# Attention on one core: a third pair of score banks for the first 15 ticks, key remainders and early normalisation on GpSimd

## The reference

```python
H_l = H @ W_l
H_r = H @ W_r
S = H_l @ H_r.T
beta = jax.nn.softmax(S, axis=-1)
B = beta @ H
O = B @ W_h @ W_g
return adj @ H + gamma * O
...
x = _layernorm(x + _L3_gnn_ref(x, adj, ...), axis=-1)
```

## Time and profile before

| what | us |
|---|---|
| median of three runs | 1487.05 |
| the profiled execution: its own time | 1489.51 |
| its span, first to last instruction | 1487.7 |
| PE busy in the span | 1383.7 (93%) |
| DVE busy | 901.8 (61%) |
| ACT busy | 690.0 (46%) |
| GpSimd busy | 235.3 (16%) |

### The profile page before, as it was taken

One profiled execution on the slowest core, in us unless ns is written; L12 is line 12 of the kernel. 1 busy time (PEld: TensorE's weight loads), 2 busy tenths in 40 slices (PEclk: granted clock), 3 DMA queues, 4 the chain that ended last, 5 costly groups with the idle time before them and its releaser, 6 DMA issues.

```text
span 1487.7 us, 17011 instructions
## 1 busy us (share of the span) xinstructions
PE 1383.7 (93%) x5831; PEld 792.1 (53%) x5831; DVE 901.8 (61%) x1223; ACT 690.0 (46%) x871; POOL 235.3 (16%) x136
## 2 busy tenths in 40 slices
PE   5999999988899989989999999999799999999995
PEld 2444444422122223237777767777567676667753
DVE  2767666700000013358888887776888888888875
ACT  0100010111001102247777766665687887788776
POOL 0111111000000000001011000000233333333343
PEclk8999999999999999999999999999999999999998
DMA  9966655699999999998899988985000000000001
GB/s 347 356 242 253 236 226 226 209 373 408 407 403 409 408 404 406 408 373 296 309 325 315 315 294 299 318 301 196 0 1 1 1 1 1 1 1 1 1 1 57
DMA packets 101296, 339.40 MB, mean 228 GB/s; under 512 B 11371, under 2 KB 12907, under 8 KB 101099
## 3 DMA queue, kind: packets, MB, share of 16 engines
q1 hardware_dynamic: 101226, 338.50, 61.0%
HBM read 336.36 MB, written 2.10 MB: 228 GB/s over the span
## 4 chain that ended last, share of the span: by engine, by line
PE 58%; DVE 17%; DMA 14%; ACT 6%; issue 5%; SPq 1%; POOL 0%; DVEq 0%; ACTq 0%; POOLq 0%
DMA raw<-in_adj_s 13%; PE acc L1109 8%; PE acc L1170 6%; PE acc L1165 6%; PE acc L1166 6%; PE acc L1073 5%; PE acc L1193 4%; PE acc L1093 4%; DVE peak L858 4%; DVE rsum L686 4%; PE acc L1258 3%; DVE ring L882 3%; ACT ring L612 2%; ACT ring L600 2%; DVE t_lo L791 2%
## 5 line engine op out<-in xcount | busy, mean ns | idle before, releaser
L791 DVE TENSOR_TENSOR t_lo<-raw,t_hi 128x1024 fp32r<-128x1024 f32 x224 | 275.4, 1251 | 63.7 <-ACT t_hi L555 58.9
L555 ACT ACTIVATE t_hi<-raw 128x1024 fp32r<-128x1024 f32 x224 | 234.1, 1057 | 75.2 <-PE acc L1170 71.3
L1165 PE MATMUL acc<-t_hi,st_hi 128*128 128x512 f32 x448 | 201.7, 450 | 4.2 <-DVE st_lo L696 2.9
L476 POOL TENSOR_TENSOR ring_lo<-ring,p_hi 128x1024 fp32r<-128x1024 f32 x64 | 155.4, 2429 | 271.4 <-ACT p_hi L606 271.4
L1109 PE MATMUL acc<-raw,h_a 128*20 128x512 f32 x736 | 163.9, 607 | 20.5 <-DMA raw<-in_adj_s 20.3
L1073 PE MATMUL acc<-raw,x 128*128 128x512 f32 x384 | 177.1, 610 | 6.2 <-DMA raw<-in_adj_s 6.2
L500 ACT ACTIVATE at<-acc 128x512 f32<-128x512 f32 x48 | 28.7, 597 | 317.9 <-PE acc L1109 184.9
L1166 PE MATMUL acc<-t_hi,st_lo 128*128 128x512 f32 x448 | 175.4, 392 | 0.0
L722 DVE TENSOR_TENSOR xs<-e,bias 128x512 f32<-128x512 f32 x8 | 5.5, 691 | 275.1 <-PE e L989 275.1
L882 DVE TENSOR_TENSOR ring<-ring,e 128x1024 f32<-128x1024 f32 x128 | 154.4, 1212 | 0.1
L600 ACT ACTIVATE ring<-ring 128x1024 f32<-128x1024 f32 x128 | 134.7, 1054 | 37.0 <-DVE ring L882 36.9
(11 more groups left out here) (181 smaller groups left out, 2105.4 us busy)
## 6 DMA issues: line engine op xcount, KB each, us to landing
raw<-in_adj_s SPq DMA_DIRECT2D x584, 512.0 KB, 6.8
resident<-in_adj_s SPq DMA_DIRECT2D x16, 512.0 KB, 7.7
raw<-in_adj_s SPq DMA_DIRECT2D x24, 256.0 KB, 8.0
kept_t<-in_adj_s SPq DMA_DIRECT2D x8, 512.0 KB, 6.2
x<-in_x SPq DMA_DIRECT2D x4, 512.0 KB, 8.1
x<-in_x SPq DMA_DIRECT2D x1, 2048.0 KB, 15.6
kept_s<-in_adj_s SPq DMA_DIRECT2D x8, 256.0 KB, 6.4
kept_v<-in_adj_s SPq DMA_DIRECT2D x8, 256.0 KB, 6.6
```

Of the source, the lines that this page charges most:

```text
L476: nc.gpsimd.tensor_tensor(ring_lo[:, n % RING, :], slot(n), p_hi[:, m % 2, :].bitcast(F32), ALU.subtract).then_inc(pl_done, 1)
L555: nc.scalar.activation(t_hi[:, (par * NS + g) % HL, :], raw[:, k, :], ACT.Copy).then_inc(hi_done, 1)
L791: nc.vector.tensor_tensor(t_lo[:, k, :], raw[:, slot_no(s, c, g), :], t_hi[:, k, :].bitcast(F32), ALU.subtract).then_inc(lo_done, 1)
L1165: mm(a[:, :], block_of(st_hi, b), hi[:, m], start=(b == 0), stop=False)
```

## The change

- **Banks.** `acc0` and `acc1` become halves of one tensor `acc01`. Ticks 0 to 14 take `rs01`, `e23` and `acc01` in turn, later ones `rs01` (odd) and `e23` (even). The wait is then on tick t-3 up to tick 16, on t-2 after it. Tick 2 waits until the last sweep's `acc` is empty.
- **Key remainders** of chunks 1 to 7 go from DVE to GpSimd, ahead of its `add_one`, whose four parts follow the remainders 4, 5, 6 and 7, one after each.
- **Value splits** move five ticks back, to ticks 11 to 18 on ACT and 12 to 19 on DVE.
- **The last norm** goes in three parts. Blocks 0 to 15: variance on DVE in tick 93, square root on ACT in tick 94, scales on DVE in tick 95, and GpSimd writes three blocks behind each of the slots 75, 77, 79, 81 and two behind 83 and 85. Blocks 16 to 23: the same in ticks 123 to 125, and GpSimd writes two blocks behind each of the slots 113, 115, 117, 119. Blocks 24 to 31 at the end: DVE writes five, ACT three. GpSimd's slot n is exponentiated in ACT's tick n + 19.
- **Sums first.** `out_proj` does its four one-column products before the projection and signals them with a semaphore `l_mm`; `finish_sums` waits for that alone and `finish_add` for `out_mm`.
- **Chunk 6** is finished seven ticks later (ticks 141 to 143 in place of 134 to 136).
- SP's five result parts have new bounds: blocks 0 to 8, 9 to 15, 16 to 23, 24 to 28, 29 to 31.

```diff
-        acc = [bank("acc0"), bank("acc1")]
+        acc01 = ctx.enter_context(nc.psum_tensor("acc01", [P, PW], F32))
+        acc = [acc01[:, 0:CW], acc01[:, CW:PW]]
...
-        LN_PARTS = ((0, NB - CB), (NB - CB, NB))
-        ACT_LN = {NT + 9: (0, 4), NT + 11: (4, 8), NT + 13: (8, 12), NT + 15: (12, 16)}
-        DVE_LN = {NT + 9: (16, 19), NT + 11: (19, 22), NT + 13: (22, 25), NT + 15: (25, 28)}
-
-        RESULT = ((0, 8, 1), (16, 22, 0), (8, 16, 1), (22, 28, 0), (28, 32, 0))
+        LN_PARTS = ((0, 16), (16, 24), (24, NB))
+        LN_SCALES = (NT - 34, NT - 4)
+        POOL_LN = {NT - 53: (0, 3), NT - 51: (3, 6), NT - 49: (6, 9), NT - 47: (9, 12), NT - 45: (12, 14), NT - 43: (14, 16),
+                   NT - 15: (16, 18), NT - 13: (18, 20), NT - 11: (20, 22), NT - 9: (22, 24)}
+        LN_LAST = (NB - 2 * CB, NB - 3, NB)
+
+        RESULT = ((0, 9, "fin_xp", 1), (9, 16, "fin_xp", 2), (16, 24, "fin_xp", 3), LN_LAST[:2] + ("fin_x", 1),
+                  LN_LAST[1:] + ("fin_xa", 1))
+
+        def score_bank(t):
+
+            return (rs01, e23, acc01)[t % 3] if t < KP - 1 else (e23, rs01)[t % 2]
+
+        def same_bank_earlier(t):
+
+            if t < 3:
+                return None
+            return t - 3 if t <= KP else t - 2
...
+            for a, b, by, count in RESULT:
+                sp.wait_ge({"fin_x": fin_x, "fin_xa": fin_xa, "fin_xp": fin_xp}[by], count)
...
+            def keys_lo(c):
+                pool.wait_ge(k_hi_done, c + 1)
+                nc.gpsimd.tensor_tensor(cols(k_lo, c - 1), cols(v, c), cols(k_hi, c - 1).bitcast(F32),
+                                        ALU.subtract).then_inc(k_lo_done, 1)
+
+            def add_one(j):
+                part = cols(x, j, 2 * CW)
+                nc.gpsimd.tensor_tensor(blocks(part, NC), blocks(part, NC),
+                                        ones_f[:, :].unsqueeze(1).broadcast_to([P, NC, D]),
+                                        ALU.add).then_inc(v1_done, 1)
+
+            def normalise_first(a, b):
+                pool.wait_ge(fin_nmr, 1 if b <= LN_PARTS[0][1] else 2)
+                for n in range(a, b):
+                    i = nc.gpsimd.tensor_scalar(block_of(v, n), block_of(xf, n), rstd_a[:, n:n + 1],
+                                                nmr_a[:, n:n + 1], ALU.mult, ALU.add)
+                if b in [r[1] for r in RESULT]:
+                    i.then_inc(fin_xp, 1)
...
-            add_one()
+            pool.wait_ge(pe_acc, NC * NSWEEP)
+            pool.wait_ge(S["xb"], done("xb", 5, NC - 1))
+            for c in range(1, NC):
+                keys_lo(c)
+                if c >= NC // 2:
+                    add_one(c - NC // 2)
             for n in range(NT):
                 if n % KP in SPLIT:
                     weights_lo(n)
+                if n in POOL_LN:
+                    normalise_first(*POOL_LN[n])
...
-            def last_norm(t):
-                a, b = ACT_LN[t]
-                act.wait_ge(fin_nmr, 1)
+            def last_norm(a, b):
+                act.wait_ge(fin_nmr, 3)
                 for n in range(a, b):
                     i = nc.scalar.activation(block_of(v, n), block_of(xf, n), ACT.Identity,
                                              bias=nmr_a[:, n:n + 1], scale=rstd_a[:, n:n + 1])
-                if b in [r[1] for r in RESULT]:
-                    i.then_inc(fin_xa, 1)
+                i.then_inc(fin_xa, 1)
...
-                if 6 <= t < 6 + NSPLIT:
-                    values_hi(t - 6)
-                if t == NT + 8:
-                    last_deviation(0)
-                if t in ACT_LN:
-                    last_norm(t)
+                if 11 <= t < 11 + NSPLIT:
+                    values_hi(t - 11)
+                if t in LN_SCALES:
+                    last_deviation(LN_SCALES.index(t))
 
             ticks(tick, keys_hi)
             evacuate_weighted(GQ - 1)
-            last_deviation(1)
+            last_deviation(2)
+            last_norm(*LN_LAST[1:])
...
-                dve.wait_ge(out_mm, i + 1)
+                dve.wait_ge(l_mm, i + 1)
...
+                dve.wait_ge(out_mm, i + 1)
...
-                if 7 <= t < 7 + NSPLIT:
-                    values_lo(t - 7)
-                if i is not None and after == 2:
+                if 12 <= t < 12 + NSPLIT:
+                    values_lo(t - 12)
+                later = 7 if i == GQ - 2 else 0
+                if i is not None and after == 2 + later:
                     finish_sums(i)
-                if i is not None and after == 3:
+                if i is not None and after == 3 + later:
                     finish_add(i)
-                if i is not None and after == 4:
+                if i is not None and after == 4 + later:
                     finish_stats(i)
-                if t == NT + 8:
-                    last_variance(0)
-                    last_scales(0)
-                if t in DVE_LN:
-                    last_norm(*DVE_LN[t])
-
-            ticks(tick, keys_lo)
+                if t + 1 in LN_SCALES:
+                    last_variance(LN_SCALES.index(t + 1))
+                if t - 1 in LN_SCALES:
+                    last_scales(LN_SCALES.index(t - 1))
+
+            ticks(tick)
             finish_sums(GQ - 1)
             finish_add(GQ - 1)
             finish_stats(GQ - 1)
-            last_variance(1)
-            last_scales(1)
-            last_norm(*LN_PARTS[1])
+            last_variance(2)
+            last_scales(2)
+            last_norm(*LN_LAST[:2])
...
-                    pe.wait_ge(s_copied, t - 1)
-                    pe.wait_ge(s_maxed, t - 1)
+                if t == 2:
+                    pe.wait_ge(S["at"], done("at", 5, NC - 1))
+                if same_bank_earlier(t) is not None:
+                    pe.wait_ge(s_copied, same_bank_earlier(t) + 1)
+                    pe.wait_ge(s_maxed, same_bank_earlier(t) + 1)
                 qh, ql = q_hi[:, i % 2, :], q_lo[:, i % 2, :]
                 for u in range(2):
-                    o = s_banks[t % 2][:, u * CW:(u + 1) * CW]
+                    o = score_bank(t)[:, u * CW:(u + 1) * CW]
...
             def out_proj(i):
                 pe.wait_ge(bt_done, i + 1)
                 for b in range(CB):
-                    mm(block_of(free_banks[i % 2], b), block_of(bt, b), w_hg[:, :], start=True, stop=True)
+                    n = mm(acc[i % 2][:, b:b + 1], block_of(bt, b), ones_d[:, 0:1], start=True, stop=True)
+                n.then_inc(l_mm, 1)
                 for b in range(CB):
-                    n = mm(acc[i % 2][:, b:b + 1], block_of(bt, b), ones_d[:, 0:1], start=True, stop=True)
+                    n = mm(block_of(free_banks[i % 2], b), block_of(bt, b), w_hg[:, :], start=True, stop=True)
                 n.then_inc(out_mm, 1)
 ```

More of the change, by code:

```diff
@@ L170, in build @@
         e2, e3 = e23[:, 0:CW], e23[:, CW:PW]
[L171 removed]
+        free_banks = (e0, e1)
         def sem(name):
@@ L407, in _ @@
             chunks(sp, step)
-            for n, (a, b, by_act) in enumerate(RESULT):
-                if by_act:
-                    sp.wait_ge(fin_xa, sum(r[2] for r in RESULT[:n]) + 1)
-                else:
-                    sp.wait_ge(fin_x, sum(not r[2] for r in RESULT[:n]) + 1)
+            for a, b, by, count in RESULT:
+                sp.wait_ge({"fin_x": fin_x, "fin_xa": fin_xa, "fin_xp": fin_xp}[by], count)
                 sp.dma_start(out[:, a * D:b * D], v[:, a * D:b * D]).then_inc(out_done, 16)
@@ L460, in _ @@
             keep_old_x(5, NC - 1)
-            def add_one():
-                pool.wait_ge(pe_acc, NC * NSWEEP)
-                pool.wait_ge(S["xb"], done("xb", 5, NC - 1))
-                for c in range(NC // 2):
-                    part = cols(x, c, 2 * CW)
-                    nc.gpsimd.tensor_tensor(blocks(part, NC), blocks(part, NC),
-                                            ones_f[:, :].unsqueeze(1).broadcast_to([P, NC, D]),
-                                            ALU.add).then_inc(v1_done, 1)
+            def keys_lo(c):
[14 more added lines that the diff above has]
+                    i.then_inc(fin_xp, 1)
             def weights_lo(n):
@@ L836, in _ @@
             chunks(dve, step)
-            def keys_lo(c):
-                dve.wait_ge(k_hi_done, c + 1)
-                nc.vector.tensor_tensor(cols(k_lo, c - 1), cols(v, c), cols(k_hi, c - 1).bitcast(F32),
-                                        ALU.subtract).then_inc(k_lo_done, 1)
             def values_lo(j):
```

15 lines of the change are left out of this document (6 added, 9 removed).

## The result

Before: median 1488.37 us (6 runs, 1486.51 to 1490.28). After: 1480.18 us (6 runs, 1478.47 to 1481.04). The ratio is 0.9945, interval 0.9932 to 0.9958: 8.2 us faster, where 9.0 were forecast.

The account below looks back on a forecast made before the run. PE was taken to bound full chunks, the loop over two bank pairs the start; near the finish PE fell behind its pace. -4.3 + 3.9 + 2.3 - 11.0 + 0.1 = -9.0 from 1487.05 gave 1478.0 us, range 1470 to 1485.

Parts of the forecast that it names:

- head: Ticks 0 to 15: with three bank pairs GpSimd's remainder and `add_one` bind instead; -4.3 us, bounds -7 and 0.
- tick 94: Scales of blocks 0 to 15: table loads make PE stand 2.6 us, GpSimd delays DVE's identity scaling 1.3; +3.9.
- tick 124: Scales of blocks 16 to 23: 2.8 us on ACT brings the last fold 2.3 later; +2.3, bounds 0 and +3.
- tail: Ticks 128 to 148: only PE's pace of 3.11 us per two ticks is left; -11.0, bounds -12 and -7.
- end: Last part: early sums save 0.4 us, more blocks and one more transfer add 0.3 to 0.8; 0.1 in all.
- Norm blocks: 24 blocks moved to GpSimd, taken as 0.4 us each and hidden both in the middle and near the finish.
- rival that needed 1.4: GpSimd norm blocks far dearer: from 1.4 us each the gain is gone, at 1.8 time 1495; chance 0.07.
- Table switch with drain: Rival: a drain as long as each ACT table load makes four middle switches cost 5.1 us more, 1483; chance 0.05.

Follow-up runs that it names:

- keys on VectorE: Changed kernel with key remainders back on DVE and `add_one` in one run, three pairs of banks kept; attention 439.19 us against 440.45.
- chunk 6 early: Changed kernel with chunk 6 finished in ticks 134 to 136 as before the change; attention 444.11 us against 440.45.

## Why the prediction was right

| term | predicted | measured | how |
|---|---|---|---|
| head | -4.3 (-7 to 0) | -4.7 | rows 0 and 1 came 4.97 and 4.69 earlier |
| tick 94 | +3.9 (+1.5 to +5) | +4.0 | 55.32 - 51.36 |
| tick 124 | +2.3 (0 to +3) | +2.2 | 52.97 - 50.75 |
| tail | -11.0 (-12 to -7) | -10.8 | 33.91 - 44.70 |
| end | +0.1 (-0.4 to +0.8) | +0.7 | 11.20 - 10.52 |
| sum | -9.0 | -8.8 | 440.45 - 449.23; medians -8.2 |

The five terms make -8.6; the other -0.2 lies in the four plain chunks, 51.36 us each before and 51.32 after, which the forecast took as unchanged.

- **Head.** The loop of remainder and `add_one` was the bound, at 3.6 us per pair against 3.8: the remainder took 1.29 (1.25 assumed), `add_one` 2.40, less than the 2.55, as the remainders beside which it once ran are gone from DVE. The maximum of tick 15 came 4.95 us earlier; predicted were 5.9 less 1.2. That two pairs give back exactly the old head is shown by the experiment; that GpSimd's pace binds, and that little hangs on it, by the keys on VectorE (0.87 us gained by the pace, 0.98 where `v_lo` no longer meets `add_one`). So remainders and `add_one` in turn on GpSimd cost mostly by that collision, which I had put at 1.2 us. Not foreseen was a bound only 0.5 us per pair behind GpSimd's.
- **Tick 94.** Both of its terms came out in size: 2.54 for the loads (2.6) and 1.4 for the rest (1.3). The mechanism that I gave for the second, the three blocks that push the remainder of slot 77, describes what the rows of after show, but is not its cause in the sense that removing it helps. With the blocks out of the way the same time is lost, and another operation of DVE takes the collision. The right size of this term is thus in part luck.
- **Tick 124.** 2.26 without the loads, 2.3 predicted. PE's wait for the fold of that chunk grew from 1.71 to 2.51, and 1.20 went on another wait, for a maximum two ticks earlier. There was no collision: DVE's scales ended before the remainder began (1422.28 + 0.17, 1422.99).
- **Norm blocks** cost GpSimd 0.44 each (1.31 for three, 0.88 for two), 0.4 assumed. The rival that needed 1.4 is excluded, and they were hidden: no wait of PE for `ring_lo` in the tail.
- **Table switch with drain.** In ticks 94 and 124 load, square root, load and exponential follow each other with no gap above 0.03 us. The Trainium skill (ScalarE: Activation LUTs, section What ACT_TABLE_LOAD costs) adds some 1380 ns of drain to each load. No row here shows it, and the whole price measured by leaving the switches out is 2.3 to 2.5 us for two loads and a square root.
- **Tail.** The size was right, and the sum was made from PE's pace, so it didn't have to say which cause was worth what. When I had to say it, for chunk 6 early, I put its finish at 1 us or less; it is 3.45, and the norm's part 7.3. In the prediction both causes stand side by side and unpriced, which is why this error didn't show in it.
- **End.** The term was too low by 0.6. Sums ahead of the projection bring the last norm 0.27 us forward (6.71 in place of 6.98 behind the last product), as DVE then waits 0.62 for the projection; I had counted 0.4. Five blocks in place of four give 0.26 back:

```profile
1468.35 0.69 DVE L913 TENSOR_TENSOR o_s<-e,lg 128x512 f32<-128x512 f32 x1 [0.62 <-PE e L1287]
...
1472.21 1.37 DVE L951 TENSOR_SCALAR v<-xf,rstd_a,nmr_a 128x128 f32<-128x128 f32 x5
1473.60 0.81 SPq L424 DMA_DIRECT2D out<-v  x2
```

  The rest is the second transfer: from its first issue to the end of the span 3.1 us, where one transfer took 2.4 (issue at 1485.31, end at 1487.7).

Not foreseen at all was how cheap the other placements were. The change pays 6.2 us at two places, 4.8 of them for the switches of tables. Four ticks later the first place costs 0.35, eight ticks later 1.1, and with the other blocks behind the last tick the second costs nothing. In part this could be seen in the profile of before: in the chunk that ends in tick 95 ACT's longest waits, 2.27 us at 1299.52 and 1.56 at 1307.94, lie in the middle, and the last ten microseconds ahead of the transposes hold 1.0 (0.55, 0.26 and 0.19); behind the last tick DVE stands 12.75 us and ACT 3.40.

## What to carry to other kernels

A stall of 2.8 us on an engine with slack cost 2.5 us just ahead of a serial step (fold, transposes, row), 1.1 nine ticks ahead of the next one and 0.35 thirteen ticks ahead, so choose the tick, not only the engine. Before moving work off a bound engine, work out the period of the engine that takes it and that of the next bound. And set GpSimd's long instructions against all of VectorE's SBUF-to-SBUF instructions in the window: moving one out of the way may only let the next one meet it.
